# Second feed-forward stage of a two-layer attention kernel: ScalarE writes the rounded high part, VectorE makes the low part from the PSUM bank

## The reference

```python
xn = _layernorm(x)                       # x: 8 x 512 x 128
x  = x + L0_attn(xn) + L0_ffn(xn)        # differential attention: softmax over q1,k1 and q2,k2,
                                         # 16 heads of 4 dims each; o = attn1 - lam * attn2, RMS norm, projection
                                         # L0_ffn: 128x128 product of FP6-quantised blocks, plus bias
xn = _layernorm(x)
x  = x + L1_attn(xn) + L1_ffn(xn)        # L1_attn: 16 heads of 8 dims with rotary embedding

def L1_ffn(x):                           # weights are +1 or -1 from booleans k0, k1, k2
    h = concatenate([x, -x], axis=-1)    # 256 features
    h = relu(s0 * (h @ w(k0))) * 2       # 512 features  (stage ff0)
    h = relu(s1 * (h @ w(k1))) * 2       # 512 features  (stage ff1)
    return s2 * (h @ w(k2))              # 128 features  (stage ff2)
```

## Time and profile before

| what | value |
|---|---|
| median of 3 runs | 815.64 us |
| the profiled execution's own time | 815.69 us |
| its span (first to last instruction) | 813.9 us |
| TensorE matmul busy | 749.1 us (92%) |
| ScalarE busy | 755.6 us (93%) |
| VectorE busy | 554.7 us (68%) |
| GpSimd busy | 64.1 us (8%) |
| mean granted TensorE clock | 0.995 |

### The profile page before, as it was taken

One profiled execution on the slowest core, in us unless ns is written; L12 is line 12 of the kernel. 1 busy time (PEld: TensorE's weight loads), 2 busy tenths in 40 slices (PEclk: granted clock), 3 DMA queues, 4 the chain that ended last, 5 costly groups with the idle time before them and its releaser, 6 DMA issues.

```text
span 813.9 us, 18430 instructions
## 1 busy us (share of the span) xinstructions
PE 749.1 (92%) x6975; PEld 250.4 (31%) x6975; DVE 554.7 (68%) x1185; ACT 755.6 (93%) x847; POOL 64.1 (8%) x84
## 2 busy tenths in 40 slices
PE   8888889999999999999999999999998889999997
PEld 5122222342323223232332323232332223333332
DVE  7788786778784687757876677856877476377322
ACT  4899989999999999999999999999989899899986
POOL 4111110000020100201011010101001000000000
PEclk9899999999999999999999999999999999999999
DMA  3916435502256025440265212660353403302500
GB/s 110 196 31 157 97 99 145 128 2 78 79 121 155 14 79 136 107 110 14 92 152 135 53 53 85 144 163 1 106 130 90 120 1 128 82 1 88 133 14 14
DMA packets 46000, 74.12 MB, mean 91 GB/s; under 512 B 7360, under 2 KB 23360, under 8 KB 45776
## 3 DMA queue, kind: packets, MB, share of 16 engines
q1 hardware_dynamic: 44096, 67.31, 32.3%
q0 software_dynamic: 1744, 5.44, 2.2%
q10 hardware_dynamic: 64, 0.10, 0.0%
HBM read 36.84 MB, written 35.65 MB: 89 GB/s over the span
## 4 chain that ended last, share of the span: by engine, by line
PE 55%; ACT 25%; DVE 10%; issue 7%; DMA 2%; SPq 1%; DVEq 0%; ACTq 0%
ACT probs L858 24%; PE ps_pv L1044 23%; PE ps_s L1025 12%; PE ps_misc L883 8%; PE ps_misc L879 6%; PE ps_misc L884 5%; PE ps_misc L872 1%; SPq L576 1%; DMA k_c<-parts_dram 1%; DVE pv_sb L1607 1%; ACT ff_out L810 1%; DVE h_lo L1283 0%; DVE h_hi L1281 0%; DMA k_ab<-thirds_dram 0%; DVE tmp L1145 0%
## 5 line engine op out<-in xcount | busy, mean ns | idle before, releaser
L858 ACT ACTIVATE probs<-ps_s 128x1024 f32<-128x1024 f32 x768 | 723.0, 1062 | 27.8 <-PE ps_s L1025 26.2
L1044 PE MATMUL ps_pv<-probs,v_aug 128*32 128x512 f32 x3072 | 410.2, 606 | 6.3 <-DVE pv_sb L1607 5.6
L1025 PE MATMUL ps_s<-q_ab,k_ab 32*128 32x512 bf16 x896 | 88.4, 384 | 24.4 <-ACT probs L858 21.9
L1025 PE MATMUL ps_s<-q_c,k_c 32*128 32x512 f32 (+1 forms) x640 | 81.8, 500 | 16.6 <-ACT probs L858 16.1
L1044 PEld LDWEIGHTS ps_pv<-probs,v_aug 128*32 128x32 f32 x3072 | 61.2, 108 | 98.0 <-issue 81.6
L883 PE MATMUL ps_misc<-h_hi,k_w 128*128 128x512 f32 x192 | 87.9, 458 | 3.4 <-DVEq L1285 1.2
L884 PE MATMUL ps_misc<-h_lo,k_w 128*128 128x512 f32 x192 | 75.7, 394 | 0.0
L1607 DVE STREAM_TRANSPOSE pv_sb<-ps_pv 128x512 f32<-128x512 f32 x48 | 34.4, 717 | 56.8 <-PE ps_pv L1044 53.0
L883 PEld LDWEIGHTS ps_misc<-h_hi,k_w 128*128 128x128 f32 x192 | 35.8, 187 | 105.5 <-issue 56.2
L1025 PEld LDWEIGHTS ps_s<-q_ab,k_ab 32*128 32x128 bf16 x896 | 22.6, 91 | 144.5 <-ACT probs L858 117.3
L1025 PEld LDWEIGHTS ps_s<-q_c,k_c 32*128 32x128 f32 (+1 forms) x640 | 30.9, 182 | 109.4 <-ACT probs L858 89.5
(11 more groups left out here) (168 smaller groups left out, 619.9 us busy)
## 6 DMA issues: line engine op xcount, KB each, us to landing
parts_dram<-qk_parts SPq DMA_DIRECT2D x38, 256.0 KB, 3.0
parts_dram<-qk_parts SPq DMA_DIRECT2D x16, 512.0 KB, 2.8
q_c<-parts_dram SPq DMA_DIRECT2D x32, 256.0 KB, 5.0
k_c<-parts_dram SPq DMA_DIRECT2D x32, 256.0 KB, 7.1
thirds_dram<-qk_thirds SPq DMA_DIRECT2D x42, 192.0 KB, 2.7
q_ab<-thirds_dram SPq DMA_DIRECT2D x56, 128.0 KB, 3.2
k_ab<-thirds_dram SPq DMA_DIRECT2D x56, 128.0 KB, 3.6
thirds_dram<-qk_thirds SPq DMA_DIRECT2D x28, 128.0 KB, 2.7
```

What stands on the lines that cost most here:

```text
L858: nc.scalar.activation(probs[:, U.slot(s), 2 * half:2 * half + 2], ps_s[:, 2 * pair:2 * pair + 2], ACT.Exp, bias=-SCALE[U.layer] * BOUND[U ...
L1025: ins = nc.tensor.matmul(ps_s[:, bank, :], k[row:row + n, slot, c * P:(c + 1) * P], q[row:row + n, slot, :], start=True, stop=True)
L1044: ins = nc.tensor.matmul(ps_pv[32 * j:32 * j + 32, :], v_aug[:, U.v, c, a:a + 32], probs[:, U.slot(s), j, :], start=c == 0 and not odd, st ...
```

## The change

A new tuple `ROUNDED` names the 29 jobs of stage ff1_b that are not in `DIRECT`. For them ScalarE writes its relu straight into the high part `h1_hi` (fp32r) instead of `ff_out`, and counts `ff_split` up, not `job_taken_act`. VectorE drops its cast, makes the low part from the bank and the high part in one instruction, waits for it, and only then counts `job_taken` up. The stage ff0 stays as it was.

```diff
+ROUNDED = tuple(("ff1_b", b, f) for b in range(NSEQ) for f in range(NF) if ("ff1_b", b, f) not in DIRECT)
...
 def taker(item):
-    return "dve" if item in DIRECT else TAKER[item[0]]
+    return "dve" if item in DIRECT or item in ROUNDED else TAKER[item[0]]
...
             def job(item):
 
+                if item in ROUNDED:
+                    name, b, f = item
+                    act.wait_ge(job_made, PLAN.made[item])
+                    wait(act, ff_split, 2 * (2 * NF * b + (0 if name == "ff0" else NF) + f))
+                    nc.scalar.activation((h0_hi if name == "ff0" else h1_hi)[:, f, :], ps_misc[:], ACT.Relu).then_inc(ff_split, 1)
+                    return
                 if not is_job(item) or PLAN.taken[item][0] != "act":
                     return
...
-                if (name, b, f) in DIRECT:
-                    dve.wait_ge(job_made, PLAN.made[name, b, f])
-                    settled()
-                    nc.vector.tensor_scalar(hi, ps_misc[:], 0.0, None, ALU.max).then_inc(ff_split, 1)
+                if (name, b, f) in DIRECT or (name, b, f) in ROUNDED:
+                    if (name, b, f) in DIRECT:
+                        dve.wait_ge(job_made, PLAN.made[name, b, f])
+                        settled()
+                        nc.vector.tensor_scalar(hi, ps_misc[:], 0.0, None, ALU.max).then_inc(ff_split, 1)
                     dve.wait_ge(ff_split, n + 1)
                     nc.vector.scalar_tensor_tensor(lo, ps_misc[:], 0.0, hi.bitcast(F32), ALU.max, ALU.subtract).then_inc(ff_split, 1)
                     dve.wait_ge(ff_split, n + 2)
                     dve.sem_inc(job_taken, 1)
```

## The result

The changed kernel took 827.72 us, the median of 4 runs (826.79 to 828.58), beside 815.62 (815.22 to 815.67) of the kernel before on the same chip. The ratio is 1.0147, 95% interval 1.0134 to 1.0160: 1.5% slower, where 1.8% (830.3) was predicted. The profiled execution took 828.58 us with a span of 826.4, 12.5 more than before, at a granted clock of 0.994. So there are 12.5 us to place between the two traces.

The account below looks back on a forecast made before the run. ScalarE (93% busy) and TensorE (92%) were taken as the bound; longer bank holds cost 7.0 (batches 1 to 4) + 3.6 + 2.2 + 1.6 + 0.3 = 14.7 us, giving 830.3 us, 1.8% slower; 8-in-10 range 821 to 835.

Parts of the forecast that it names:

- d = h + 0.80 - p: Delay per tile: h is VectorE's lateness behind the relu, 0.80 low part plus count, p TensorE's next bank user's start.
- the slack: Time between next scores being ready and ScalarE wanting them: none at tile 0, 0.22 us at tile 3 of batch 2.
- tile 0 of batch 2: Steady part: h = 0.45, p = 0.62, delay 0.63 us, no slack, cost 0.63 us.
- tile 0 of batch 5: Same formula in batch 5: h = 0.99, cost 1.17 us.
- tile 3 of batch 2: Steady part, VectorE coming from the quantisation: h = 0.68, p = 0.50, delay 0.98, slack 0.22, cost 0.76 us.
- the durations of relu and low part: Relu into fp32r taken as 0.598 us; low part 0.691 from the bank against 0.692 from `ff_out`, so 0 us.
- dear relu: Rival: ScalarE's relu to fp32r takes 0.778 us, adding 5.2 us, 835.6 us in all; chance 0.08.
- ScalarE is full in between, so what it loses does not come back: Batches 1 to 4: losses of 1.76 us a batch all reach the end, 7.0 us for four.
- I count them as nothing on the path by themselves: The 29 dropped VectorE casts, 12.4 us, save nothing themselves; they only let VectorE reach a later job earlier.
- faster: Rival: the end waits for VectorE, at `ps_pv` transposes and takes of norms behind the split; 814.4 us, chance 0.05.
- Absorbed: Rival: TensorE's leads and an earlier VectorE largely absorb the delay; 6 to 9 us more, 822 to 825; chance 0.20.
- Hidden: Rival: the bank is free before TensorE gets to it, holding at one or two of 29 places; 815.6 us, chance 0.05.

Follow-up runs that it names:

- hold alone: Kernel before, keeping relu to `ff_out` and VectorE's cast, but VectorE makes the low part from the bank and frees it afterwards: 846.59 us, ratio 1.0377.
- batch 5 alone: The change made only for the four tiles of batch 5, the rest as in the kernel before: 816.67 us, ratio 1.0015.

## Why the prediction was right

- *Right, and shown:* the price of a place is when VectorE is there, plus its instruction, plus the count, less TensorE's own start (d = h + 0.80 - p), less the slack. With the measured h it gives 0.46 for tile 0 of batch 2 (measured 0.45), 0.22 for tile 1 (0.22) and 0.97 for tile 0 of batch 5 (0.97). With 0.46 us more of hold the same formula holds.
- *Luck in the sums:* tile 3 of batch 2 was given as 0.76 and measured as 0.74 to 0.76, but from h = 0.68 and a slack of 0.22, where h was 0.58 and the slack came out as some 0.13. In batch 5 tile 0 was given 0.2 too much (1.17, measured 0.97) and tile 3 0.2 too little (1.4, measured 1.57), so that 3.6 stands beside 3.53.
- *Right:* the durations of relu and low part. The dear relu did not occur (0.598, not 0.778). The Trainium skill (Perfetto Trace Analysis, Optimizing Scalar/DVE Operations) gives about 65 ns more overhead to an operation of VectorE on PSUM; after the change 38 such operations have a median of 692 ns, as the ones from SBUF had, so the page's rule is not borne out for this operation.
- *Right in kind:* the slack. In the steady part it takes nothing from tiles 0 and 1, some 0.13 from tile 3 (0.88 of delay, 0.74 to 0.76 of cost), and tile 2 lies at 0.20, at the upper end of the given 0 to 0.22.
- *Mis-sized:* tile 0 (0.63, measured 0.44 to 0.46 in batches 1 to 4). I took h over from the trace of before, but the dropped wait for the preceding instruction lets VectorE start sooner, by 0.11 by experiment. Over the steady part this, less 0.05 more at each tile 2, is why 6.4 stands under 7.0. In batch 0 tile 0 cost 0.50 and not 0.3, tile 2 0.41 and not 0.25, tile 3 0.96 and not 1.2.
- *Wrong:* the step "ScalarE is full in between, so what it loses does not come back", which the sum takes over for batch 5. It holds in batches 1 to 4 and fails in unit 19: there ScalarE waited 1.34 us for a load behind VectorE's cast, the hold at tile 3 of batch 5 delays the exponentials by 1.5 us more than that cast, and these 1.5 us come back. "I count them as nothing on the path by themselves" is wrong at the same place by 0.9 us if the casts are dropped alone, and as good as right in the changed kernel, where the cast waits for TensorE. The rival *faster* named the right kind of path; its place (`ps_pv` transposes and norms) was another, and the hold outweighed it many times over. Had I followed the idle time of 1.34 us at 640.01 back through its load, a term of some 1.5 would have stood in the sum: 14.7 - 1.5 = 13.2, and 828.9. The 0.35 us of unit 21 no reading of mine accounts for.
- *Absorbed* fell for batches 1 to 4 with the hold experiment: neither a lead of TensorE nor an earlier VectorE damps the loss there. In unit 19 something of its kind does happen, but the cover is ScalarE's wait for a load, and it takes in 1.5 us once. *Hidden* holds at one place only, batch 7 tile 0, as given (growth 0.01).

Open stay 0.07 us of tile 0, the 0.24 ahead of the first changed job, the 0.35 of unit 21, and 0.5 us in unit 19 of hold alone.

## What to carry to other kernels

Price a longer hold of a shared bank place by place: when the engine that now frees it gets there, plus its instruction, plus the count, less when the next user came; then take off the slack up to the next wait of the engine that is full. Work taken off an engine that is not full was worth nothing here at 16 places in a row, and something where a product and a transfer wait behind it; a delay, too, costs nothing where the full engine would have waited for a transfer anyway. So look for the idle gaps of the full engine, follow them back through the transfer, and try the order of the table there before moving work between engines. A pure reordering gave 0.2% here, where the change in question lost 1.5%.

## What the runs showed of the hardware

- One more semaphore wait on VectorE's queue, on a count reached long before, moved the start of the next instruction from 0.03 to 0.10 us behind its release, at all of the on-time places.
- Near the start of the program TensorE stands for some 7 us at the 1.2 GHz level in some executions (granted 0.50 from 24 to 27 us and 0.75 from 17 to 24 in before's trace) and not in others of the same kernel (1.00 in both stretches in the repeat of the changed kernel). Other traces have a shorter such stretch elsewhere: batch 5 alone between 60 and 75 us (0.93 on average), hold alone from 643 to 646 us (0.51). The one at the start is worth about 2 us in the span, more than most of the single terms above.
- GpSimd cast a 128x512 tile to fp32r in 0.61 us where VectorE took 0.43, and subtracted in 1.28 where VectorE took 0.69. Where GpSimd's cast and subtraction (0.93 and 1.61 us) ran beside two instructions of VectorE that read SBUF tiles, these took 0.98 and 1.59 us and not 0.69.
